# Reordered start of a fused image filter, transformer and attention kernel: loads, one tanh, and a step of VectorE's hand-written order

## The chip, the cores and the metric

The kernel runs on one core of a Trainium2 chip. A core has TensorE (PE in the profile, its weight loads PEld), VectorE (DVE), ScalarE (ACT), GpSimd (POOL) and SyncE (SP, which here only issues transfers). The metric is the time of one launch on the device in microseconds, the median of several runs.

## The reference, cut to what matters

Eight images of 256x256 go through ten iterations of a filter (`_L0_tok_ref`), eight token sequences of 128 go through a four-layer transformer (`_L0_txt_ref`), and the two results are joined and go through a windowed attention and a feed-forward block with spike counts. Only the first two concern the change. The filter, with `conv` meaning differences of neighbouring rows and columns:

```
u = sigmoid(o / EPS); q = 0
for _ in range(10):
    u_nabla = conv(u, nabla_w)
    q = maximum(q - TAU * (u_nabla[:, 0] * vf1 + u_nabla[:, 1] * vf0), 0)
    Tq = conv(stack([vf1 * q, vf0 * q]), div_w)
    u = sigmoid((o - Tq) / EPS)
return (o - Tq) / EPS
```

The transformer starts with `h = emb[x] + positional_encoding`. Each of its four blocks is softmax attention over 16 heads of width 16, a layer norm, a feed-forward part of width 1024 and a layer norm.

## The kernel before

Every engine has its own instruction list, written out by hand as a sequence of small named functions; semaphores tie the lists together. An engine works strictly in the order of its list, so a function whose inputs are late holds up all that stands behind it. That written order is what sets the order of the work everywhere in this case. There is no scheduler.

The images are handled in four pairs, two images at a time spread over 128 partitions with four rows each (`RPP`). One filter iteration `it` is this chain: ScalarE computes `u = tanh(...)` in `filter_out` (or `first_tanh` for the first iteration of a pair); VectorE takes column differences (`columns_apart`, L1715), weighs them with one component of the vector field (`columns_weighed`, L1721), takes row differences (`rows_apart`, L1726), advances q (`advance_columns`, L1739 in a pair's first iteration and L1743 later), weighs the rows (`rows_weighed`, L1732), and then does `advance_rows` (L1748), `flux_rows` (L1754), `flux_cols` (L1760), `divergence_columns` (L1765), `divergence_rows` (L1770), `divergence_both` (L1775) and `divergence_out` (L1779), which releases the next tanh. Rows that lie on another partition are fetched by small SBUF to SBUF copies on SP's queue: `rows_below` (L271) for u after each tanh, `rows_above` (L318) for the flux. `rows_apart` waits for the first, `divergence_rows` for the second.

The transformer runs 16 blocks, four layers by four pairs of sequences. Block k's attention (`a`) is interleaved with the feed-forward part of block k-1 (`f`) in `block_step`, and two filter iterations are woven into each block. The first block has no feed-forward part to go with and a list of its own, `first_step`, on each engine. In the attention, TensorE makes transposed h (`turn_attn`, L531), ScalarE copies it (`attn_in`, L1127), TensorE projects it (L546), ScalarE copies keys and queries (`keys_out`, `queries_out`, L1163), TensorE makes scores for two sets of 8 heads at a time (`scores`, L597), VectorE reduces each set to its maxima (`head_max(k, n)`, n = 0 to 3, L1784), ScalarE exponentiates (`exps(k, n, half)`, L1100), TensorE transposes the probabilities (`turn_probs`, L607) and multiplies by the values (`attend`, L619), VectorE takes `reciprocals` (L1788) of the sums, ScalarE spreads and copies them (`spread_rden`, `rden_out` L1121), VectorE multiplies (`normalise`, L1793), and TensorE projects the result out (`project_out`, L636). `scores(0, 1)` may start only when `exps(0, 1, 1)` is done. The next block begins with VectorE's `columns_apart`, `columns_weighed`, `moments_attn` (statistics of what `project_out` left) and `head_max(a, 0)`.

In the prologue SP loads tokens, the first images (`o_all`), and the vector field `vf` in two components: component 1, with which the columns are weighed (`l_vf`), and component 0, for the rows (`l_vf_rows`). ScalarE issues the loads of the filter taps and of the positional encoding `pe`. VectorE compares the taps with the expected ones and branches on the outcome. GpSimd gathers embedding rows into `h`: two gathers at once, then it waits for the projection weights `w_attn` (`l_qkv`) before the other six. When all gathers have landed (`g_emb`) SP issues the remaining weights of the first layer (`first_weights`, among them `w1` of 1 MB), and behind them in its list stands `rows_below(1)`.

At the end of a pair ScalarE writes the finished pair scaled by 0.5 to `f_out` (L1090), then computes the first tanh of the next pair from `o_all` (L1081).

## Time and profile before

| what | value |
|---|---|
| median of 3 runs | 996.21 us (996.08 to 999.59) |
| the profiled execution: its own time, its span | 997.71 us, 996.0 us |
| busy share of the span: PE, DVE, ACT, POOL | 92%, 84%, 70%, 12% |
| mean granted TensorE clock | 0.972 of full |
| chain that ended last, by engine | DVE 45%, PE 26%, ACT 17%, issue 8% |
| stretch of the first block (start to the third iteration's first difference) | 0 to 58.4 us |

The span runs from the first to the last instruction of the profiled execution; its own time is a little longer. A granted clock of 1 is 2.4 GHz, of 0.5 is 1.2 GHz. The busy share of PE is that of pipelined matmuls with modelled ends and does not mean that it runs at its peak. In rows of the timeline an end is start plus duration; two instructions of an engine can overlap by about 0.1 us, since the next starts while the last one's results drain.

### The profile page before, as it was taken

The page shows a single profiled execution, that of the slowest core. Times are in us where ns is not written, and L with a number is a line of the kernel's source. Part 1 is how long each engine was busy: PE and PEld are TensorE (multiplying, and loading weights), DVE is VectorE, ACT ScalarE, POOL GpSimd, SP SyncE. Part 2 cuts the span into 40 slices and gives each one's busy share as a digit, 9 for nine tenths or more (in the row PEclk, how much of TensorE's full clock was granted, in tenths as well). Part 3 has the DMA queues.
Part 4 walks back from the last instruction along what each step waited for, and adds up shares of the span by engine and source line. Part 5 has one row for each costly group of instructions (what it writes and reads, how often), then busy time and mean ns, then how long its engine had stood idle before and what let it go on. Part 6 is the DMA issues. An engine that isn't in the chain of part 4 may idle for free.

```text
span 996.0 us, 18934 instructions
## 1 busy us (share of the span) xinstructions
PE 912.3 (92%) x6988; PEld 708.9 (71%) x6988; DVE 833.2 (84%) x1160; ACT 699.2 (70%) x2252; POOL 119.2 (12%) x147
## 2 busy tenths in 40 slices
PE   6689999999999999989999999889998999999997
PEld 5467777777777777877777877767675766667675
DVE  4889999999999999999999998888799599452443
ACT  2766877876877877877876875757767686867842
POOL 4301011011011111101101111101011101000000
PEclk8699999999999999999999999799999999999999
DMA  5312030031010120010220010000001000100000
GB/s 141 91 72 61 32 112 17 27 117 48 17 43 17 45 81 35 17 47 13 70 80 11 17 38 11 12 11 23 27 17 35 20 23 11 49 27 2 17 1 32
DMA packets 24924, 39.00 MB, mean 39 GB/s; under 512 B 4000, under 2 KB 20608, under 8 KB 23552
## 3 DMA queue, kind: packets, MB, share of 16 engines
q1 hardware_dynamic: 24016, 36.59, 11.6%
q0 software_dynamic: 384, 1.05, 0.6%
q8 instruction: 56, 0.92, 0.4%
q14 instruction: 36, 0.29, 0.1%
q10 hardware_dynamic: 432, 0.15, 0.1%
HBM read 22.21 MB, written 5.24 MB: 28 GB/s over the span
## 4 chain that ended last, share of the span: by engine, by line
DVE 45%; PE 26%; ACT 17%; issue 8%; DMA 2%; POOL 1%; SPq 0%; DVEq 0%; POOLq 0%; ACTq 0%
ACT prob L1100 8%; PE ps_t L857 6%; PE ps_m L868 4%; DVE f L1775 4%; DVE f L1779 4%; DVE f L1748 4%; DVE f L1770 4%; DVE neg_max L1784 4%; DVE p L1760 4%; ACT u L1087 3%; DVE f L1765 3%; DVE f L1715 2%; DVE f L1732 2%; DVE f L1743 2%; DVE f L1721 2%
## 5 line engine op out<-in xcount | busy, mean ns | idle before, releaser
L1100 ACT ACTIVATE prob<-ps_s,neg_max 128x128 f32<-128x128 f32 x512 | 181.1, 406 | 3.3 <-DVE neg_max L1784 3.3
L1100 ACT ACTIVATION_READ_ACCUMULATOR prob<-ps_s,neg_max 128x1 f32 x512 | 126.1, 247 | 0.0
L661 PE MATMUL ps_t<-w,hidT 128*128 128x256 f32 x512 | 125.7, 383 | 0.0
L1108 ACT ACTIVATE probT<-ps_t 128x512 f32<-128x512 f32 x128 | 80.9, 632 | 47.5 <-PE ps_t L607 30.9
L661 PEld LDWEIGHTS ps_t<-w,hidT 128*128 128x128 f32 x512 | 91.0, 190 | 12.1 <-ACT hidT L1184 2.6
L857 PE MATMUL ps_t<-km,w_fc 128*128 128x384 f32 x256 | 91.6, 492 | 1.4 <-ACT km L1299 1.4
L607 PE MATMUL ps_t<-ident,prob 128*128 128x128 f32 x512 | 82.7, 286 | 8.9 <-ACT probT L1108 5.0
L607 PEld LDWEIGHTS ps_t<-ident,prob 128*128 128x128 f32 x512 | 61.5, 146 | 31.4 <-issue 13.0
L1784 DVE TENSOR_REDUCE neg_max<-ps_s 128x8 f32<-128x1024 f32 x64 | 77.5, 1212 | 3.8 <-PE ps_s L597 3.8
L1358 ACT ACTIVATE prob<-ps_s,neg_max 128x128 f32<-128x128 f32 x192 | 53.9, 376 | 26.2 <-DVE neg_max L1965 25.8
L650 PE MATMUL ps_t<-hT_f,w 128*128 128x256 f32 x256 | 65.7, 402 | 3.0 <-ACT hT_f L1112 3.0
L546 PE MATMUL ps_s<-hT_a,w_attn 128*128 128x256 f32 x256 | 66.8, 396 | 1.5 <-DMA w_attn<-in_w_attn 1.5
L857 PEld LDWEIGHTS ps_t<-km,w_fc 128*128 128x128 f32 x256 | 46.2, 190 | 26.1 <-ACT km L1299 1.9
L868 PE MATMUL ps_m<-w_pr,o_all 128*128 128x256 f32 x256 | 63.8, 385 | 0.0
L1715 DVE TENSOR_TENSOR f<-u 128x1024 f32<-128x1024 f32 x40 | 48.9, 1223 | 16.1 <-ACT u L1087 12.4
L1087 ACT ACTIVATE u<-f 128x1024 f32<-128x1024 f32 x36 | 38.1, 1057 | 34.2 <-DVE f L1779 34.1
L650 PE MATMUL ps_y<-hT_f,w 128*128 128x256 f32 x256 | 60.6, 379 | 0.0
L650 PEld LDWEIGHTS ps_t<-hT_f,w 128*128 128x128 f32 x256 | 50.1, 201 | 12.9 <-ACT hT_f L1112 6.1
L1142 ACT ACTIVATE h<-ps_y,shift_a,rstd_a 128x256 f32<-128x256 f32 x32 | 16.3, 562 | 55.4 <-DVE shift_a L1817 55.4
L546 PEld LDWEIGHTS ps_s<-hT_a,w_attn 128*128 128x128 f32 x256 | 46.6, 197 | 9.9 <-issue 3.2
L868 PEld LDWEIGHTS ps_m<-w_pr,o_all 128*128 128x128 f32 x256 | 46.1, 190 | 8.5 <-issue 1.0
L1726 DVE TENSOR_TENSOR f<-u 128x1024 f32<-128x1024 f32 x40 | 48.9, 1222 | 3.7 <-DMA u<-u 3.4
(179 smaller groups left out, 2046.1 us busy)
## 6 DMA issues: line engine op xcount, KB each, us to landing
w<-in_w SPq DMA_DIRECT2D x8, 1024.0 KB, 5.0
u<-u SPq DMA_DIRECT2D x80, 63.0 KB
p<-p SPq DMA_DIRECT2D x80, 63.0 KB
w_attn<-in_w_attn SPq DMA_DIRECT2D x4, 768.0 KB, 4.7
out<-w SPq DMA_DIRECT2D x7, 384.0 KB, 2.6
o_all<-in_o SPq DMA_DIRECT2D x4, 512.0 KB, 4.7
filtered<-f_out SPq DMA_DIRECT2D x4, 512.0 KB, 3.1
x<-filtered SPq DMA_DIRECT2D x8, 256.0 KB, 2.7
```

The lines of the kernel that those rows point to most:

```text
L546: last = mm(dst, w_attn[:, c, D * w + P * m:D * w + P * m + P], hT_a[:, k % 2, c], start=(c == 0), stop=(c == KC - 1))
L607: last = tr(ps_t[:, 1, P * hh:P * hh + P], prob[:, n % 2, 4 * half + hh], ident[:])
L650: last = mm(ff_banks[j % 2][:, D * (m % 2):D * (m % 2) + D], w1[:, c, P * m:P * m + P], hT_f[:, c], start=(c == 0), stop=(c == KC - 1))
L661: last = mm(ps_t[:, 0, D * t:D * t + D], hidT[:, m, P * t:P * t + P], w2[:, m], start=False, stop=(m == MC - 1), skip_group_check=True)
L857: last = mm(ps_t[:, m % 2, 0:TOK], w_fc[:, c, P * m:P * m + P], xn2T[:, c], start=(c == 0), stop=(c == KC - 1))
L868: last = mm(dst, hid_f[:, m, P * t:P * t + P], w_pr[:, m], start=(m == 0), stop=(m == MC - 1))
L1087: A(u[:, 0:RPP, 0:IMG], fa, ACT.Tanh, scale=0.25).then_inc(s["act_tanh"], 1)
L1100: last = A(prob[:, n % 2, hh], ps_s[n % 2][:, hh], ACT.Exp, scale=-1.0, bias=neg_max[:, n % 2, hh:hh + 1], accum_out=den)
L1108: A(probT[:, 4 * half:4 * half + 4].rearrange("p h k -> p (h k)"), ps_t[:, 1], ACT.Copy).then_inc(s["act_pT"], 1)
L1358: last = A(prob[:, t % 2, head], quad[hb][:, P * hh:P * hh + P], ACT.Exp, bias=neg_max[:, t, head:head + 1])
L1715: tt(fb, u[:, 0:RPP, 1:], u[:, 0:RPP, 0:IMG], ALU.subtract).then_inc(s["u_cols"], 1)
L1784: dve.tensor_reduce(neg_max[:, n % 2], ps_s[n % 2][:], AX.X, ALU.min).then_inc(s["dve_max"], 1)
```

## The change

Five edits, none of which changes what is computed or how many arithmetic instructions there are:

1. The two tap loads and the load of `pe` go from ScalarE's list to SP's: the taps stand ahead of the images, `pe` behind component 1 of the field.
2. The load of the projection weights `w_attn` stands ahead of component 0 of the field (the row field), no longer behind the first row copies.
3. ScalarE's explicit wait for GpSimd's constants ahead of the first tanh is gone.
4. In `first_step`, VectorE's `divergence_columns(0)` goes ahead of `head_max(0, 0)`; the first half of the second iteration (`columns_weighed(1)`, `rows_apart(1)`, `advance_columns(1)`) goes ahead of `head_max(0, 2)` and `head_max(0, 3)`; the two `normalise` go behind the whole divergence. ScalarE's `filter_out(0)` goes between the two halves of `exps(0, 1)`.
5. At the end of a pair the next pair's first tanh is computed before the copy to `f_out`. `rows_apart` of a pair's first iteration, which overwrites what the copy reads, gets a wait for the copy.

```diff
@@ -259,11 +259,20 @@
             sp.dma_start(tokens[:], d["tokens"]).then_inc(s["l_tok"], 16)
+            sp.dma_start(taps[:, 0:18], d["nabla_w"].partition_broadcast(P)).then_inc(s["l_taps"], 16)
+            sp.dma_start(taps[:, 18:36], d["div_w"].partition_broadcast(P)).then_inc(s["l_taps"], 16)
             load_images = lambda k: sp.dma_start(o_all[:, k], d["o"][2 * k:2 * k + 2].rearrange("b (p r) c -> (b p) r c", r=RPP))
             load_images(0).then_inc(s["l_img"], 16)
-            for comp, loaded in ((1, "l_vf"), (0, "l_vf_rows")):
+
+            def load_field(comp, loaded):
                 for img in range(2):
-                    sp.dma_start(vf[64 * img:64 * img + 64, comp], d["vf"][comp].rearrange("(p r) c -> p r c", r=RPP)).then_inc(s[loaded], 16)
+                    sp.dma_start(vf[64 * img:64 * img + 64, comp], d["vf"][comp].rearrange("(p r) c -> p r c", r=RPP)).then_inc(loaded, 16)
+
+            load_field(1, s["l_vf"])
+            sp.dma_start(pe[:], d["pe"]).then_inc(s["l_pe"], 16)
+            sp.dma_start(w_attn[:, :, 0:3 * D], d["w_attn"][0][:, :, 0:3 * D]).then_inc(s["l_qkv"], 16)
+            load_field(0, s["l_vf_rows"])
+
...
             sp.wait_ge(s["c_pool"], N_EARLY)
             rows_below(0)
-            sp.dma_start(w_attn[:, :, 0:3 * D], d["w_attn"][0][:, :, 0:3 * D]).then_inc(s["l_qkv"], 16)
...
-            act.dma_start(taps[:, 0:18], d["nabla_w"].partition_broadcast(P)).then_inc(s["l_taps"], 16)
-            act.dma_start(taps[:, 18:36], d["div_w"].partition_broadcast(P)).then_inc(s["l_taps"], 16)
-            act.dma_start(pe[:], d["pe"]).then_inc(s["l_pe"], 16)
...
                 else:
-                    act.wait_ge(s["st_img"], 16 * pair + 16)
-                    A(f_out[:], fa, ACT.Copy, scale=0.5).then_inc(s["act_img"], 1)
                     if pair + 1 < PAIRS:
                         act.wait_ge(s["l_img_rest"], 16 * (PAIRS - 1))
                         first_tanh(pair + 1)
+                    act.wait_ge(s["st_img"], 16 * pair + 16)
+                    A(f_out[:], fa, ACT.Copy, scale=0.5).then_inc(s["act_img"], 1)
...
                 exps(0, 1, 0)
+                filter_out(0)
                 exps(0, 1, 1)
                 probs_out(0, 1, 0)
-                filter_out(0)
                 probs_out(0, 1, 1)
...
-            act.wait_ge(s["c_pool"], N_EARLY)
             act.wait_ge(s["l_img"], 16)
             first_tanh(0)
...
             def rows_apart(it):
                 dve.wait_ge(s["act_tanh"], it + 1)
                 dve.wait_ge(s["halo_u"], 32 * it + 32)
+                if it and it % ITERS == 0:
+                    dve.wait_ge(s["act_img"], it // ITERS)
...
                 flux_cols(0)
+                divergence_columns(0)
                 head_max(0, 0)
-                divergence_columns(0)
                 head_max(0, 1)
...
                 columns_apart(1)
-                head_max(0, 2)
-                head_max(0, 3)
                 columns_weighed(1)
                 rows_apart(1)
                 advance_columns(1)
+                head_max(0, 2)
+                head_max(0, 3)
                 rows_weighed(1)
+                advance_rows(1)
                 reciprocals(0, 0)
-                advance_rows(1)
-                reciprocals(0, 1)
                 flux_rows(1)
                 flux_cols(1)
+                reciprocals(0, 1)
                 divergence_columns(1)
-                normalise(0, 0)
                 divergence_rows(1)
-                normalise(0, 1)
                 divergence_both(1)
                 divergence_out(1)
+                normalise(0, 0)
+                normalise(0, 1)
                 restart()
```

What the edits do to the compiled lists is shown at three places. First ScalarE's list from its start, before, with what each instruction waits for (`l_img` is the landing of the first images, `c_pool` GpSimd's constants):

```order
L1072 UNCONDITIONAL_BRANCH [waits barrier_Pool_Activation_PE_DVE_SP_release]
L1076 DMA taps<-in_nabla_w 128x18
L1077 DMA taps<-in_div_w 128x18
L1078 DMA pe<-in_pe 128x256
L1081 ACT_TABLE_LOAD [waits l_img]
L1081 ACTIVATE u<-o_all 128x4x256 [waits c_pool]
L1275 TENSOR_LOAD general [waits c_general]
```

And the same place in the changed kernel, where the first tanh is line 1085:

```order
L1080 UNCONDITIONAL_BRANCH [waits barrier_Pool_Activation_PE_DVE_SP_release]
L1085 ACT_TABLE_LOAD
L1085 ACTIVATE u<-o_all 128x4x256 [waits l_img]
L1278 TENSOR_LOAD general [waits c_general]
L1278 ISA x2
```

With two waits the compiler put that for the images on the table load and that for the constants on the tanh; with one wait it stands on the tanh, and the table load waits for nothing.

Second, SP's list from its start, before:

```order
L261 DMA tokens<-in_tokens 128x8
L262 DMA o_all<-in_o 128x1024
L266 DMA vf<-in_vf 64x1024 x4
L271 DMA u<-u 63x256 x2
L275 DMA w_attn<-in_w_attn 128x2x768
```

And in the changed kernel:

```order
L261 DMA tokens<-in_tokens 128x8
L262 DMA taps<-in_nabla_w 128x18
L263 DMA taps<-in_div_w 128x18
L264 DMA o_all<-in_o 128x1024
L269 DMA vf<-in_vf 64x1024 x2
L272 DMA pe<-in_pe 128x256
L273 DMA w_attn<-in_w_attn 128x2x768
L269 DMA vf<-in_vf 64x1024 x2
L280 DMA u<-u 63x256 x2
```

Two small loads now stand ahead of the images, and the projection weights stand ahead of two of the four field loads and of the row copies.

Third, VectorE's list in the first step, from the second iteration's column differences on, before (`f` is any of the filter's work tiles):

```order
L1715 TENSOR_TENSOR f<-u 128x1024
L1784 TENSOR_REDUCE neg_max<-ps_s 128x8 x2
L1721 TENSOR_TENSOR f<-f,vf 128x1024
L1726 TENSOR_TENSOR f<-u 128x1024
L1743 SCALAR_TENSOR_TENSOR f<-f 128x1024
L1732 TENSOR_TENSOR f<-f,vf 128x1024
```

And in the changed kernel, where these lines are 3 to 5 higher:

```order
L1718 TENSOR_TENSOR f<-u 128x1024
L1724 TENSOR_TENSOR f<-f,vf 128x1024
L1731 TENSOR_TENSOR f<-u 128x1024
L1748 SCALAR_TENSOR_TENSOR f<-f 128x1024
L1789 TENSOR_REDUCE neg_max<-ps_s 128x8 x2
L1737 TENSOR_TENSOR f<-f,vf 128x1024
```

The two maxima of the third and fourth head sets moved behind the row differences and the advance of the columns.

## Rows read from the trace of the kernel before

**Rows 1.** The page: shares by engine of the chain that ended last.
```profile
DVE 45%; PE 26%; ACT 17%; issue 8%; DMA 2%; POOL 1%; SPq 0%; DVEq 0%; POOLq 0%; ACTq 0%
```

**Rows 2.** That chain, 0 to 130 us: start us, us, what.
```profile
12.39 4.63 DMA w_attn<-in_w_attn
...
17.15 5.99 PE ps_s L546 x16
...
31.08 1.40 ACT prob L1100 x8
...
57.33 1.06 ACT u L1087
```

**Rows 3.** Timeline, 0 to 17 us: start us, us, engine line operation, idle before.
```profile
8.21 1.28 ACT L1081 ACT_TABLE_LOAD   x1 [8.21 <-DMA o_all<-in_o]
...
15.72 0.60 ACT L1127 ACTIVATE hT_a<-ps_s 128x512 f32<-128x512 f32 x1 [5.16 <-PE ps_s L531]
...
11.93 1.23 DVE L1721 TENSOR_TENSOR f<-f,vf 128x1024 f32<-128x1024 f32 x1
...
13.96 0.69 DVE L1704 TENSOR_TENSOR h<-h,pe 128x512 f32<-128x512 f32 x1
...
14.71 0.92 PE L531 MATMUL ps_s<-ident,h 128*128 128x128 f32 x4 [4.57 <-DVE h L1704]
```

**Rows 4.** Transfers issued at 2.3 (last of two), 7.1 and 30.9 us: last number us to landing.
```profile
vf<-in_vf SPq DMA_DIRECT2D x2, 256.0 KB, 7.7
...
h<-in_emb,tok_idx POOLq DMA_INDIRECT x1, 6.1
...
w<-in_w SPq DMA_DIRECT2D x1, 1024.0 KB, 6.1
```

**Rows 5.** Timeline, 25 to 39 us, SP, ACT and DVE.
```profile
28.73 0.61 SPq L344 DMA_DIRECT2D w_attn<-in_w_attn  x1
...
38.82 0.37 ACT L1100 ACTIVATE prob<-ps_s,neg_max 128x128 f32<-128x128 f32 x1 [0.47 <-DVE neg_max L1784]
...
25.03 1.23 DVE L1784 TENSOR_REDUCE neg_max<-ps_s 128x8 f32<-128x1024 f32 x1 [3.85 <-PE ps_s L597]
...
36.42 1.23 DVE L1715 TENSOR_TENSOR f<-u 128x1024 f32<-128x1024 f32 x1 [2.42 <-ACT u L1087]
37.57 2.35 DVE L1784 TENSOR_REDUCE neg_max<-ps_s 128x8 f32<-128x1024 f32 x2
```

**Rows 6.** Timeline, 49 to 62 us, ACT, DVE and PE.
```profile
52.83 0.42 ACT L1121 ACTIVATE rden<-ps_s 128x256 f32<-128x256 f32 x1
...
61.77 1.19 DVE L1784 TENSOR_REDUCE neg_max<-ps_s 128x8 f32<-128x1024 f32 x1
...
55.10 1.89 PE L636 MATMUL ps_y<-w_attn,attnT 128*128 128x256 f32 x8
58.92 1.74 PE L597 MATMUL ps_s<-km,qT 32*128 32x256 f32 x16 [1.93 <-ACT qT L1163]
```

**Rows 7.** The chain again, at a row copy that ended a wait.
```profile
613.76 1.06 ACT u L1087
...
615.58 2.19 DMA u<-u
```

**Rows 8.** Timeline, 198 to 216 us, at the end of the first pair.
```profile
203.63 1.06 ACT L1090 ACTIVATE f_out<-f 128x1024 f32<-128x1024 f32 x1 [0.93 <-DVE f L1779]
...
204.60 1.04 ACT L1081 ACTIVATE u<-o_all 128x1024 f32<-128x1024 f32 x1
...
205.74 1.23 DVE L1715 TENSOR_TENSOR f<-u 128x1024 f32<-128x1024 f32 x1 [1.41 <-ACT u L1081]
```

**Rows 9.** Waits of DVE, 57 to 560 us: us in total, times, longest.
```profile
DVE f L1715 <- ACT u L1081: 2.7, 2, 1.4
```

**Rows 10.** Sums over stretches: us, PE busy (instructions), granted clock, DMA share, GB/s.
```profile
15.00:21.80 6.80, 5.28 (x15) 0.50 0.31 100
...
618.00:640.00 22.00, 17.98 (x156) 0.77 0.02 7
```

## The prediction

> **What bounds the kernel now.** I read the page first, for the engines' shares of the chain that ended last: VectorE has 45% of it and TensorE 26% [rows 1], so neither alone is the limit, and a reordering counts only where the chain runs through what it moves. I then followed the chain in order of time. In the prologue it goes through transfers: the first images, the tanh, the projection weights (landed at 12.39 + 4.63 = 17.02), the projections at 17.15 [rows 2]. In the first block it goes to the third head set's maxima and the exponentials behind them, then through ScalarE and TensorE, and at 57.33 to the tanh of the second iteration [rows 2], 4 us later than ScalarE could have computed it, since its copy of the sums was done at 52.83 + 0.42 = 53.25 [rows 6]. From there on, through the text blocks, it is mostly VectorE's own list with a tanh between iterations. So a lead that all three engines have at the start of block 1 is carried to the end, and a lead of VectorE alone is not. That is what I work out: at what time the three can start block 1.
>
> **The prologue.** ScalarE's table load waits for the images and takes 1.28 us (8.21 to 9.49) ahead of the tanh [rows 3]; in the changed list it waits for nothing and is over long before. The images are issued two tap loads later, some 0.9 us (I estimate this from SP's 0.4 to 0.6 us for an issue, such as the 0.61 of [rows 5]), but no longer share the engines with the taps and `pe`; I take 8.6 instead of 8.2 for their landing (bounds 8.2 and 9.1), so the tanh ends at 9.7 and the column differences start at 9.75. Weighing them needs component 1 of the field. Its two parts landed on average 7.7 us after issues up to 2.3 [rows 4], the later one thus at 10.0 or after; it too is issued 0.9 later, so I take 11.3 (bounds 10.0 and 12.2). From the start of that weighing to `positions_first` is 13.96 - 11.93 = 2.03 us of VectorE's work [rows 3]: 11.3 + 0.05 + 2.03 = 13.4. The second gather landed at 7.15 + 6.1 = 13.25 [rows 4] and nothing of it is moved, which gives the same 13.4. So `positions_first` gains about 0.55 us, not the 1.3 of the table load.
>
> From `positions_first` to the projections are 0.75 us to the transposes, 1.01 to the copy, 0.60 for it and 0.05: 15.72 + 0.60 + 0.05 - 13.96 = 2.41 [rows 3], that is 15.8, if the weights are there. Before they were issued at 12.39; now at about 5, behind 1 MB of images and field and `pe`. Alone they took 4.6 us [rows 2]. I estimate 14.0: before, the same queue had finished images and both components by about 12.6, and the weights put 0.25 MB more in the place of the row component and start 0.9 later (bounds 13.0 and 15.5, both before 15.8). So the projections start at 15.8 and not at 17.15: 1.35 us gained. The row component now lands behind the weights, near 16; `rows_weighed(0)` stands 2.3 us behind `positions_first`, at 15.8, and VectorE had 3.85 us of idle time ahead of the first maxima [rows 5] that hide a delay of it, less the 1.2 that `divergence_columns(0)` now takes of them and the 0.8 by which TensorE gained more than VectorE. Cover left is 1.8 us.
>
> **The first step's list.** The first maxima start at 25.03 - 1.35 = 23.7 [rows 5]. `divergence_columns(0)` lies in idle time ahead of them, so the divergence is complete at 23.7 + 2 x 1.15 + 3 x 1.25 = 29.75. ScalarE's first half of `exps(0, 1)` ended at 31.08 + 1.40 = 32.48 [rows 2], now at 31.1, and the tanh follows at once and ends at 32.1, where before it let VectorE start only at 36.42 [rows 5]. The price is a tanh (1.05) ahead of the other half of these exponentials; TensorE's `scores(0, 1)` wait for them, but end near 35.5, and their maxima are not asked for before 37.4.
>
> What asks for them late is the new order on VectorE. `rows_apart(1)` needs the row copies. Where such a copy ended a wait, it landed at 615.58 + 2.19 = 617.77, 2.95 us after its tanh ended at 614.82 [rows 7]. So VectorE works 2.5 us on the columns, idles 0.45, starts the row differences at 32.1 + 2.95 = 35.05, and after two operations of 1.2 the third set's maximum at 37.4 (before 37.57 [rows 5]). The exponentials behind it start at 38.65 instead of 38.82. Of the 1.35 us of lead 0.2 is left here: the new order spends the rest.
>
> It comes back at the end of the step. The exponentials keep ScalarE and TensorE in turn until the second copy of the sums at 53.25 - 0.2 = 53.05 [rows 6]. VectorE meanwhile ends the maxima at 39.7 and does the eight remaining operations of the iteration and the two reciprocals, waiting once for exponentials and once for the flux's row copies, by about 50.2, all in time in which it waited before. So the tanh runs from 52.95 to 54.0 instead of ending at 58.39 [rows 2], and the column differences start at 54.05 (before 58.42): 4.4 us for VectorE. The `normalise` pair, put behind the divergence, finds VectorE idle and waits only for ScalarE's copies, as before. TensorE's `project_out` starts at 54.9 (before 55.10), held by the work ahead of it; the scores can follow after 1.82 at 56.7, since the queries are copied by 54.6; before, they waited for that copy until 58.92 [rows 6]. They take 1.15 us at full clock, as at other block starts, or 1.74 as here [rows 6], and end at 57.9 or 58.4. VectorE is through column weights and statistics at 57.8. So block 1's first maxima start at 57.9 and not at 61.77 [rows 6]: 3.9 us gained, 3.4 with the slower scores. I take 3.9, as TensorE no longer idles ahead of them. The next wait there, ScalarE's for the layer norm's shift, depends on VectorE and moves with it, and so does TensorE behind that: all three have the lead.
>
> **The pair ends.** Copy and tanh ran from 203.63 to 205.64, and VectorE, idle for 1.41 us, started at 205.74 [rows 8]. It was free at 204.33; a tanh that starts at 203.63 and takes 1.04 lets it start at 204.74: 1.0 gained. The copy's end stays at 205.7, and `rows_apart`, which now waits for it, stands at 209 or later, so that wait costs nothing; if it had to follow the tanh at once it would cost 1.0. The queries' copy on ScalarE keeps its place behind both. VectorE waited so at two pair ends, 2.7 us in all [rows 9]; at the third the list of waits has no such entry, and I count nothing. That is 2.0 us.
>
> **The sum.** 3.9 + 2.0 = 5.9 us. Against the profiled execution (997.71 with a span of 996.0) that is 991.8; that execution lies 1.5 above the median, so for the median 996.21 - 5.9 = 990.3.
>
> **A rule that speaks against the change.** The row copies of the second iteration are now asked for at 32.1, not at 36.3, and `first_weights` puts `w1` on the same queue ahead of them. Before, these loads started at 28.73 [rows 5], 11.7 us after the projection weights had landed, and `w1` landed at 30.9 + 6.1 = 37.0 [rows 4], 20.0 us after them. With 14.0 for the weights that gives 25.7 and 34.0, a us before the row copies land in my sum. So I charge nothing; each us that the weights land after 15 costs one. The Trainium skill, DMA: Bandwidth & Descriptors, section Queues, rings and completion order, says that on each DMA engine descriptors are consumed in ring order. By that rule nothing overtakes `w1`, and the rival below is as dear as I price it; were the copies free to overtake, it would cost nothing.
>
> **Rivals.** (a) The forecast, chance 0.50: 990.3, own range 988.8 to 992.0. (b) The prologue gives nothing, because field, gather or weights land late, 0.15: the exponentials then start 1.15 later than before, the block start gains 3.9 - 1.35 = 2.55, and with 2.0 the time is 991.7. For it: only 0.55 us of the table load's 1.28 passes my own estimates of landings. Against it: the weights waited at 17.02 for nothing but their late issue. (c) The lead at block 1 is lost again, because TensorE has its own full list there, 0.10: only the pair ends count, 994.2. Against it: the chain before goes through VectorE there. (d) The row copies stand behind `w1`, 0.07: if it lands at 37.0 as before, they land some 3.3 late, and 993.6 is left. (e) The same mechanism makes the kernel slower, 0.05: from a landing of the copies at 41 on (35.05 + 5.9) the maxima behind them eat the whole gain, at 42 the time is 997.2; the weights would have to land later than they did before. (f) More is gained, 0.13: the granted clock was 0.50 from 15 to 21.8 [rows 10], and the 16 projections took 5.99 us [rows 2]; at full clock 8 of the same kind take 1.89 [rows 6], so 16 about 3.8. With TensorE less idle ahead of them 2.2 more may come: 988.1. The same clock works the other way too: from 618 to 640 it was 0.77 [rows 10] where TensorE bounds, and a few us at half clock more or fewer there move the time by 1 to 2 us; this is in the ranges.
>
> **How the numbers follow.** About 0.5% (5 us) is what a measurement of this kernel can tell from no change; the bound is 991.2. Of (a) three quarters lie under it, all of (f) and a third of (b): 0.375 + 0.13 + 0.05 = 0.555 for faster, rounded to 0.56. Only a part of (e) is over 1001: 0.02. The rest, 0.42, is within. The range from 987.2 to 994.6 holds (a) to (c) but for tails, most of (d) and of (f), and leaves out (e).
>
> **What would show it.** In the changed profile: the table load in the first 3 us; the projections at 15.8; the first tanh of block 0's filter ending at 32 with a VectorE wait for a row copy behind it; the third set's maximum near 37.4; the second tanh ending at 54.0; the maxima of block 1 at 57.9; no wait of VectorE for ScalarE of over 1.2 us at the pair ends. I would be wrong if the row copies landed later than 35.5, if the weights landed after 15.8, or if the difference at 58 us were not found again at 560.

## The result and the profile after

| | median | executions |
|---|---|---|
| changed kernel | 993.77 us | 12 |
| kernel before, on the same chip | 996.62 us | 12 |
| ratio | 0.9953, 95% interval 0.9935 to 0.9970 | |

By the ratio the change saves 4.7 us of 996.6 (3.0 to 6.5): by the bound of 0.5% it lies just inside "no change", and the interval shows that there is one. The two medians lie only 2.9 us apart, a little outside that interval; here and in the runs below the ratio, which has the interval, gives 0.5 to 2.2 us more than the difference of the medians. The forecast was 5.9 us. The profiled execution of the changed kernel took 995.07 us with a span of 993.3, that of before 997.71 with 996.0.

The page's shares of the chain that ended last have hardly moved from [rows 1]:

```profile
DVE 46%; PE 25%; ACT 16%; issue 9%; DMA 2%; POOL 1%; SPq 0%; DVEq 0%; POOLq 0%; ACTq 0%
```

What the change does shows in the timeline of its prologue (start us, us, engine line operation, idle before), beside [rows 3]:

```profile
0.80 1.28 ACT L1085 ACT_TABLE_LOAD   x1 [0.80 <-PEq L2245]
...
4.56 0.60 SPq L273 DMA_DIRECT2D w_attn<-in_w_attn  x1
...
7.21 1.06 ACT L1085 ACTIVATE u<-o_all 128x1024 f32<-128x1024 f32 x1 [5.13 <-DMA o_all<-in_o]
...
9.68 1.23 DVE L1724 TENSOR_TENSOR f<-f,vf 128x1024 f32<-128x1024 f32 x1 [0.16 <-DMA vf<-in_vf]
...
14.30 0.69 DVE L1707 TENSOR_TENSOR h<-h,pe 128x512 f32<-128x512 f32 x1 [2.62 <-DMA h<-in_emb,tok_idx]
...
16.39 1.22 DVE L1731 TENSOR_TENSOR f<-u 128x1024 f32<-128x1024 f32 x1 [1.39 <-DMA u<-u]
```

The table load is over at 2.08, the tanh starts at 7.21 (before 9.51), the column field is there at 9.7 and not at the expected 11.3. All of this lead is then spent in one wait: `positions_first` (L1707) waits 2.62 us for a gather and starts at 14.30, later than the 13.96 of before. The chain that ended last goes through that gather now, and not through the weights as in [rows 2] (start us, us, what):

```profile
5.95 8.28 DMA h<-in_emb,tok_idx
...
16.46 6.72 PE ps_s L554 x16
...
33.94 0.77 SPq L280
...
34.75 2.18 DMA u<-u
```

The gather was issued 1.2 us earlier than before and took 8.28 us where [rows 4] have 6.1. The projections start at 16.46 (before 17.15) and take 6.7 us, 0.7 longer than before; by the granted clock, TensorE is at half clock for 6.8 us there in both traces, before from 15.0 to 21.8 and now from 15.7 to 22.5, so that only the last 0.7 us of the projections (before 1.3) ran at full clock. The first step in the timeline, beside [rows 5] and [rows 6]:

```profile
25.07 2.35 DVE L1789 TENSOR_REDUCE neg_max<-ps_s 128x8 f32<-128x1024 f32 x2 [0.81 <-PE ps_s L605]
...
32.84 1.08 ACT L1091 ACTIVATE u<-f 128x1024 f32<-128x1024 f32 x1
...
37.02 1.22 DVE L1731 TENSOR_TENSOR f<-u 128x1024 f32<-128x1024 f32 x1 [0.53 <-DMA u<-u]
...
39.30 2.35 DVE L1789 TENSOR_REDUCE neg_max<-ps_s 128x8 f32<-128x1024 f32 x2
40.55 0.37 ACT L1104 ACTIVATE prob<-ps_s,neg_max 128x128 f32<-128x128 f32 x1 [1.42 <-DVE neg_max L1789]
...
54.13 0.42 ACT L1125 ACTIVATE rden<-ps_s 128x256 f32<-128x256 f32 x1
...
54.40 1.10 ACT L1091 ACTIVATE u<-f 128x1024 f32<-128x1024 f32 x1
...
59.44 1.23 DVE L1789 TENSOR_REDUCE neg_max<-ps_s 128x8 f32<-128x1024 f32 x1
```

The first maxima start where they did before (25.07 against 25.03), the third set's 1.7 us later than before, and block 1's 2.3 us earlier. The end of the first pair, beside [rows 8]:

```profile
201.12 1.06 ACT L1085 ACTIVATE u<-o_all 128x1024 f32<-128x1024 f32 x1 [0.93 <-DVE f L1784]
202.09 1.04 ACT L1097 ACTIVATE f_out<-f 128x1024 f32<-128x1024 f32 x1
202.28 1.23 DVE L1718 TENSOR_TENSOR f<-u 128x1024 f32<-128x1024 f32 x1 [0.46 <-ACT u L1085]
```

VectorE's idle time there fell from 1.41 to 0.46. The list of its waits from 57 to 560 us has 0.9 us in the place of the 2.7 of [rows 9] (us in total, times, longest):

```profile
DVE f L1718 <- ACT u L1085: 0.9, 2, 0.5
```

A good way to see where a lead is won and lost is to subtract the start of the same instruction in two traces. I took VectorE's maxima in the text blocks and, from 658 us on, one addition in each window of the later part. Lead over before in us, at before's time; the last column is the difference of the spans:

```
                      25    38    62   209   393   430   597   658   880   end
changed              0.0  -1.7   2.3   3.5   5.0   4.5   4.5   6.9   4.4   2.7
e1_prologue          1.2   1.2   1.4   1.4   1.7   1.8   1.9   1.8   1.8   1.8
e2_first_step       -0.6  -3.4  -0.4  -0.2   0.7   0.9   0.9   1.5  -1.2  -1.2
e3_pair_ends         0.3   0.3   0.3   1.3   2.7   2.9   2.9   5.0   0.7   0.7
e4_again             1.0  -0.3   2.6   3.7   5.6   5.8   5.8   7.1   4.9   5.0
e5_weights_behind   -0.7  -2.4   0.1   1.2   2.9   3.1   3.1   4.3   2.2   2.2
e6_weights_wait     -0.8  -2.5   1.3   2.4   2.6   2.8   2.8   5.3   5.1   5.1
e7_maxima_early      1.0   1.6   5.0   6.1   6.2   6.4   6.3   8.9   8.7   8.7
e8_both              0.2   0.7   4.1   5.2   6.5   5.8   5.8   8.2   5.7   4.0
e9_early_again       1.2   1.8   5.3   6.3   8.2   7.7   7.7   8.2   5.4   5.4
e10_early_wait_field 0.5   0.5   4.1   5.2   6.8   7.3   7.2   7.4   4.5   4.5
```

Behind 600 us no edit has changed anything, yet the leads move by up to 4.3 us between two columns, and by up to 2.7 from 597 us to the end. TensorE's clock goes with it: from 600 to 640 us the granted clock was 0.87 before and 0.91 in the changed kernel, whose lead grows by 2.4 us until 658; that the one makes the other is not shown. The changed kernel's lead falls from 6.6 us at 835 to 4.4 at 880, where its clock was below full and before's was not. Sums over 836 to 848 us (PE, weight loads, VectorE, ScalarE and GpSimd busy, granted clock, DMA share, GB/s), first the changed kernel:

```profile
836.00:848.00 12.00, 9.88 (x57) 6.03 (x58) 9.45 (x18) 8.43 (x22) 0.39 (x2) 0.72 0.27 98
```

and the same stretch of the kernel before:

```profile
836.00:848.00 12.00, 9.33 (x71) 6.14 (x69) 11.02 (x17) 9.31 (x18) 2.79 (x2) 1.00 0.03 13
```

So one profile against another can't size an edit of 1 us from the end of the program. I read leads at 62, 209, 393 and 597 us, and total times from ratios. Even there the table has noise: from 209 to 386 us, where no edit differs, the leads moved by -0.9 (e6, e7) to +0.9 us (e2, e4).

### The profile page after: what moved, and what is told of

Read it like the earlier page. It is cut to its first block, busy times and chain, and to the rows that moved or that the text cites. A ratio compares the mean times of both kernels' runs of the same rounds, so it can differ in the third digit from the quotient of the medians.

```text
span 993.3 us, 18933 instructions
## 1 busy us (share of the span) xinstructions
PE 911.6 (92%) x6988; PEld 705.3 (71%) x6988; DVE 833.9 (84%) x1160; ACT 699.0 (70%) x2252; POOL 122.2 (12%) x147
## 4 chain that ended last, share of the span: by engine, by line
DVE 46%; PE 25%; ACT 16%; issue 9%; DMA 2%; POOL 1%; SPq 0%; DVEq 0%; POOLq 0%; ACTq 0%
ACT prob L1104 8%; PE ps_t L865 6%; DVE f L1753 4%; DVE neg_max L1789 4%; PE ps_m L876 4%; DVE f L1780 4%; DVE f L1784 4%; DVE f L1775 4%; DVE p L1765 4%; ACT u L1091 3%; DVE f L1770 3%; DVE f L1748 2%; DVE f L1718 2%; DVE f L1737 2%; DVE f L1724 2%
## 5 line engine op out<-in xcount | busy, mean ns | idle before, releaser
L865 PE MATMUL ps_t<-km,w_fc 128*128 128x384 f32 x256 | 95.1, 508 | 1.0 <-ACT km L1302 1.0
L615 PE MATMUL ps_t<-ident,prob 128*128 128x128 f32 x512 | 82.0, 284 | 10.1 <-ACT probT L1112 5.1
L554 PE MATMUL ps_s<-hT_a,w_attn 128*128 128x256 f32 x256 | 67.5, 400 | 0.8 <-ACT hT_a L1131 0.8
L658 PE MATMUL ps_t<-hT_f,w 128*128 128x256 f32 x256 | 62.1, 386 | 3.8 <-ACT hT_f L1116 3.8
L1091 ACT ACTIVATE u<-f 128x1024 f32<-128x1024 f32 x36 | 38.1, 1059 | 32.8 <-DVE f L1784 32.4
L658 PEld LDWEIGHTS ps_t<-hT_f,w 128*128 128x128 f32 x256 | 47.3, 190 | 13.2 <-ACT hT_f L1116 7.4
L554 PEld LDWEIGHTS ps_s<-hT_a,w_attn 128*128 128x128 f32 x256 | 47.1, 199 | 9.0 <-issue 3.0
L1780 DVE TENSOR_TENSOR f<-f 128x1024 f32<-128x1024 f32 x40 | 48.9, 1222 | 3.7 <-issue 0.3
```

Source lines behind the costliest of these rows:

```text
L554: last = mm(dst, w_attn[:, c, D * w + P * m:D * w + P * m + P], hT_a[:, k % 2, c], start=(c == 0), stop=(c == KC - 1))
L615: last = tr(ps_t[:, 1, P * hh:P * hh + P], prob[:, n % 2, 4 * half + hh], ident[:])
L658: last = mm(ff_banks[j % 2][:, D * (m % 2):D * (m % 2) + D], w1[:, c, P * m:P * m + P], hT_f[:, c], start=(c == 0), stop=(c == KC - 1))
L865: last = mm(ps_t[:, m % 2, 0:TOK], w_fc[:, c, P * m:P * m + P], xn2T[:, c], start=(c == 0), stop=(c == KC - 1))
L1091: A(u[:, 0:RPP, 0:IMG], fa, ACT.Tanh, scale=0.25).then_inc(s["act_tanh"], 1)
L1780: tt(fa, fa, fb, ALU.add).then_inc(s["div_rc"], 1)
```

## The experiments

### The change in three parts

**e1_prologue** has edits 1 to 3 (loads, table load) in the kernel before, and nothing else.

```diff
+            sp.dma_start(taps[:, 0:18], d["nabla_w"].partition_broadcast(P)).then_inc(s["l_taps"], 16)
...
+            load_field(1, s["l_vf"])
+            sp.dma_start(pe[:], d["pe"]).then_inc(s["l_pe"], 16)
+            sp.dma_start(w_attn[:, :, 0:3 * D], d["w_attn"][0][:, :, 0:3 * D]).then_inc(s["l_qkv"], 16)
+            load_field(0, s["l_vf_rows"])
...
-            act.wait_ge(s["c_pool"], N_EARLY)
```

> Only edits 1 to 3 (loads and the wait ahead of the first tanh), the order of the first step and of the pair ends as before. Theory (after the result): the second gather gates positions_first near 14.3 and the projections run at half clock, so the first maxima start at 25.0 +- 0.7, block 1's first maxima at 61.8 +- 0.7 (before 61.77) and the time does not move by over 1 us on that account. Rival: the prologue carries a good part of the gain and the first step only passes it on; then block 1's first maxima start 1.3 us or more earlier.

Measured: 996.70 beside 997.79 us, ratio 0.9982 (0.9968 to 0.9996): 1.8 us. VectorE's rows of its timeline show the same late gather:

```profile
13.94 0.69 DVE L1707 TENSOR_TENSOR h<-h,pe 128x512 f32<-128x512 f32 x1 [2.22 <-DMA h<-in_emb,tok_idx]
...
23.84 1.22 DVE L1787 TENSOR_REDUCE neg_max<-ps_s 128x8 f32<-128x1024 f32 x1 [1.20 <-PE ps_s L605]
```

TensorE's rows show a quicker set of projections:

```profile
16.56 5.38 PE L554 MATMUL ps_s<-hT_a,w_attn 128*128 128x256 f32 x16 [0.75 <-ACT hT_a L1131]
```

The projections start 0.6 us earlier than before, not 1.35. That the maxima gain 1.2 is due to 5.38 us of projections in place of 5.99. Block 1's maxima start at 60.34, 1.4 us earlier than before: my expectation of 61.8 +- 0.7 missed, and the rival's 1.3 us is there, 0.6 of it from the quicker projections.

**e2_first_step** has edit 4 alone, in the kernel before.

```diff
                 exps(0, 1, 0)
+                filter_out(0)
                 exps(0, 1, 1)
...
-                head_max(0, 2)
-                head_max(0, 3)
                 columns_weighed(1)
                 rows_apart(1)
                 advance_columns(1)
+                head_max(0, 2)
+                head_max(0, 3)
```

> Only edit 4 (VectorE's order and the tanh amid the exponentials in the first step). The weights are then issued at 28.7 as before and w1 lands at 37.0, while the row copies of the second iteration are asked for near 33.5. Theory (ring order): the copies stand behind w1 and land at 37.7 to 38.5 instead of 36.4, so that the third set's maximum starts near 40.5 and block 1's first maxima at 60.5 to 61.0, a lead of only about 1 us where the whole change has 2.3. Rival: the copies overtake w1, land 3.0 us after the tanh near 36.4, and the lead is 2.5 to 3 us.

Measured: 997.57 us, ratio 0.9990 (0.9971 to 1.0008): nothing that can be told from noise. The new order has no lead at block 1 without the early weights (-0.4 us, expected about 1), and the trace says why. Its chain, at the row copies of the second iteration:

```profile
33.06 0.96 ACT u L1087
...
34.84 3.71 DMA u<-u
```

and its timeline on SP and VectorE:

```profile
30.96 0.43 SPq L348 DMA_DIRECT2D w<-in_w  x1
...
38.65 1.22 DVE L1726 TENSOR_TENSOR f<-u 128x1024 f32<-128x1024 f32 x1 [2.06 <-DMA u<-u]
```

The last of the row copies took 3.71 us from its issue, and landed 4.5 us after the tanh's end (34.02), where the changed kernel has 2.18 and 3.0. `w1` was issued at 30.96 and took 7.2 us, until 38.1; the copies, issued at 34.04, landed just behind it. That is rival (d), in the kernel where it applies. VectorE waits 2.06 us, the maxima behind the copies start at 40.93, 3.4 us later than before, and block 1 has no lead left. The Trainium skill (DMA: Bandwidth & Descriptors, section Queues, rings and completion order) says that each DMA engine consumes a queue's descriptors in ring order, though a later one may finish its write before an earlier one; this trace agrees with the order, 38.1 for `w1` and 38.6 for the copies behind it.

**e3_pair_ends** has edit 5 alone.

```diff
-                    act.wait_ge(s["st_img"], 16 * pair + 16)
-                    A(f_out[:], fa, ACT.Copy, scale=0.5).then_inc(s["act_img"], 1)
                     if pair + 1 < PAIRS:
                         act.wait_ge(s["l_img_rest"], 16 * (PAIRS - 1))
                         first_tanh(pair + 1)
+                    act.wait_ge(s["st_img"], 16 * pair + 16)
+                    A(f_out[:], fa, ACT.Copy, scale=0.5).then_inc(s["act_img"], 1)
...
+                if it and it % ITERS == 0:
+                    dve.wait_ge(s["act_img"], it // ITERS)
```

> Only edit 5 (the next pair's tanh ahead of the copy, a wait of rows_apart for the copy). Theory: nothing differs until 203 us; from there the lead is 1.0 us, from the second pair end on 2.0, at the third nothing is added. VectorE's wait for ScalarE at these two ends falls from 1.4 to 0.4 us. Rival: the wait for the copy holds up rows_apart, and the lead at 400 us is under 1 us.

Measured: 995.68 us, ratio 0.9974 (0.9957 to 0.9990): 2.6 us. Its lead grows by 1.0 at 206 us (0.3 to 1.3) and by 1.0 at 390 (1.7 to 2.7), and by nothing at the third pair end at 575 (2.9 before it and behind it). This term stood in the forecast at 2.0.

**e4_again** is the changed kernel once more, in the same series.

> The changed kernel itself once more, for a second trace. Theory: up to 620 us the starts agree with the first trace within 0.7 us, block 1's first maxima at 59.4; what differs behind that comes with stretches of half clock of TensorE in the fusion part, and moves the end by up to 3 us either way. Rival: the lead of 4.5 us at 600 us is itself luck of the first trace; then the two traces differ by over 1.5 us at 600 us already.

Measured: 992.79 us, ratio 0.9938 (0.9915 to 0.9961): 6.2 us, where the first measurement had 4.7. The three parts alone make 1.8 + 1.0 + 2.6 = 5.4 us. At block 1, where only the first two and their meeting count, they have 1.4 - 0.4 = 1.0 and the whole has 2.3 and 2.6: the two need each other. The clock in the projections differs between these traces, so count from the first maxima: block 1's follow 36.7 us later before, 36.5 in e1 and in e2, and 34.4 and 35.1 in the two traces of the changed kernel. The trace of this execution has the first maxima at 24.04 and the third set's at 37.84, near my 23.7 and 37.4, and still block 1 starts at 59.18. TensorE's clock takes the difference. Its timeline here:

```profile
47.28 1.09 PE L615 MATMUL ps_t<-ident,prob 128*128 128x128 f32 x4
48.30 1.08 PE L627 MATMUL ps_s<-probT,v 128*32 128x128 f32 x16
49.31 1.91 PE L554 MATMUL ps_s<-hT_a,w_attn 128*128 128x256 f32 x4
```

and in the first profile of the changed kernel:

```profile
48.73 1.09 PE L615 MATMUL ps_t<-ident,prob 128*128 128x128 f32 x4
49.75 0.67 PE L627 MATMUL ps_s<-probT,v 128*32 128x128 f32 x16
50.34 1.13 PE L554 MATMUL ps_s<-hT_a,w_attn 128*128 128x256 f32 x4
```

The same 20 matmuls end at 51.2 and 51.5, though one started 1.45 us before the other. The windows around them show the granted clock (columns as above), in the second measurement:

```profile
48.00:50.00 2.00, 2.00 (x20) 1.20 (x19) 1.86 (x3) 0.72 (x2) 0.00 (x0) 0.50 0.99 416
50.00:52.00 2.00, 2.00 (x11) 1.69 (x10) 0.70 (x1) 0.42 (x2) 0.00 (x0) 0.77 0.43 174
```

and in the first:

```profile
50.00:52.00 2.00, 2.00 (x26) 1.54 (x19) 1.97 (x2) 0.64 (x2) 0.00 (x0) 1.00 0.97 401
```

From 50 us on the first ran at full clock and the second, for a while yet, at half.

### Why the second gather is late

**e5_weights_behind** puts the weights behind component 0 of the field. I had blamed the weights for the late gather.

```diff
             sp.dma_start(pe[:], d["pe"]).then_inc(s["l_pe"], 16)
+            load_field(0, s["l_vf_rows"])
             sp.dma_start(w_attn[:, :, 0:3 * D], d["w_attn"][0][:, :, 0:3 * D]).then_inc(s["l_qkv"], 16)
-            load_field(0, s["l_vf_rows"])
```

> The changed kernel with the projection weights issued behind the row component of the field (still ahead of the row copies). Theory: in the changed kernel the weights share the DMA engines with the second gather, which landed at 14.2 us although it was issued 1.2 us earlier than before; with the field there instead it lands at 12 to 13.3, the weights at 14.5 to 15.5, the projections start at 15.0 to 15.7 (changed kernel 16.5 to 16.7), and block 1's first maxima come 0.8 to 1.3 us earlier. Rival: what delays the gather is the load on the DMA engines whatever is loaded (2.4 MB in the first 15 us in either order); then the second gather lands near 14 again and the projections start at 16.3 to 16.7.

Measured: 995.51 beside 997.59 us, ratio 0.9966 (0.9942 to 0.9991); one of its ten executions took 2278.68 us, which the ratio leaves out and for which I have no cause. The gather did not come earlier, but later:

```profile
14.69 0.69 DVE L1707 TENSOR_TENSOR h<-h,pe 128x512 f32<-128x512 f32 x1 [2.98 <-DMA h<-in_emb,tok_idx]
```

So my theory in that form is wrong: it is not the weights as such. The same bytes are on the DMA engines in another order, and the gather waits as long. The projections start at 17.30, later even than the rival had it.

**e6_weights_wait** lets SP wait for both gathers before it issues the weights and component 0; all else is the changed kernel.

```diff
             sp.dma_start(pe[:], d["pe"]).then_inc(s["l_pe"], 16)
+            sp.wait_ge(s["g_emb_first"], 32)
             sp.dma_start(w_attn[:, :, 0:3 * D], d["w_attn"][0][:, :, 0:3 * D]).then_inc(s["l_qkv"], 16)
```

> The changed kernel in which SP waits for the first two gathers before it issues the projection weights and then the row component. Theory: with nothing but the column component beside them the gathers land at 10.5 to 12, positions_first starts with them, and the weights, issued then, land about 4 us later at 15 to 16: the projections start near 15.5. Rival: the gathers take their 7 to 8 us from issue to landing for another reason than the traffic, and land at 13.5 to 14 again.

Measured: 992.65 us in one execution, span 990.9. Its timeline:

```profile
5.94 0.95 POOL L434 DMA_INDIRECT h<-in_emb,tok_idx  x1 [0.30 <-issue]
...
10.10 0.60 SPq L274 DMA_DIRECT2D w_attn<-in_w_attn  x1
...
15.52 6.09 PE L555 MATMUL ps_s<-hT_a,w_attn 128*128 128x256 f32 x16 [2.63 <-DMA w_attn<-in_w_attn]
...
18.08 1.22 DVE L1732 TENSOR_TENSOR f<-u 128x1024 f32<-128x1024 f32 x1 [5.91 <-DMA u<-u]
...
25.87 2.35 DVE L1790 TENSOR_REDUCE neg_max<-ps_s 128x8 f32<-128x1024 f32 x2
```

The gather issued at 5.94 had landed when SP went on, at 10.1: some 4.1 us, where it took 8.28 with 1.25 MB issued about it (the weights at 4.56, the row field from 5.21). The issues of both gathers (KB, median us to landing), first in this run and then in the changed kernel:

```profile
h<-in_emb,tok_idx POOLq DMA_INDIRECT x2, 4.6
```

```profile
h<-in_emb,tok_idx POOLq DMA_INDIRECT x2, 8.1
```

With e5 this settles what delayed them: load from another queue, whatever it carries. The Trainium skill (the same page and section) says that a DMA engine takes turns between the queues that have work for it, a packet at a time; a transfer that was issued first is by that rule not served alone. The first gather of the changed kernel agrees with it: issued at 4.43, just ahead of the weights, it took 7.9 us, and 5.1 in e6. The projections start 0.9 us earlier than in the changed kernel, though they now wait 2.63 us for the weights. But the row copies, last in SP's queue, end a wait at 18.08 (in the changed kernel at 16.39), and VectorE needs 7.8 us from there to the first maxima: they start 0.8 us later than before. VectorE's rows are late next.

### What the late maxima cost

**e7_maxima_early** keeps the changed kernel but for the third and fourth head sets' maxima, which go ahead of the row differences.

```diff
                 columns_weighed(1)
+                head_max(0, 2)
+                head_max(0, 3)
                 rows_apart(1)
                 advance_columns(1)
-                head_max(0, 2)
-                head_max(0, 3)
```

> The changed kernel with head_max(0, 2) and head_max(0, 3) ahead of rows_apart(1) and advance_columns(1) (behind columns_weighed(1)). Theory: in the changed kernel the third set's maximum waits behind the row copies and costs 1.8 us of ScalarE's idle time; here it starts right behind scores(0, 1), 1.5 to 1.9 us earlier relative to the first maxima, and block 1's first maxima come as much earlier, since VectorE still ends the iteration before ScalarE is free. Rival: the exponentials then run before VectorE has the divergence, the tanh waits for it, and the gain at block 1 is under 0.7 us.

Measured: 991.57 beside 997.59 us, ratio 0.9930 (0.9903 to 0.9957). Block 1's maxima start at 56.76, 2.4 us earlier than in the second trace of the changed kernel, whose first maxima start at nearly the same time (24.04, here 24.00). Part of these 2.4 us are the matmuls at half clock shown above for e4: counted from the first maxima, block 1 follows after 32.8 us here and after 34.4 in the first trace of the changed kernel, so the order is worth 1.6 to 2.4 us. The four matmuls of L554 behind the exponentials take 1.13 us in all four traces with early maxima and in the first of the changed kernel, but 1.91 in e4 and 2.08 in e5; whether the late maxima have a part in that half clock was not tried. The maxima wait for their scores now and for nothing else:

```profile
35.99 2.36 DVE L1789 TENSOR_REDUCE neg_max<-ps_s 128x8 f32<-128x1024 f32 x2 [1.01 <-PE ps_s L605]
```

**e8_both** joins this with the load order of e5.

> Both: weights behind the row component and the maxima ahead of the rows. Theory: the two gains add, 2.5 to 3 us at block 1's first maxima against the changed kernel, and the time is 0.7 to 0.8% under the kernel before. Rival: one limit takes the place of the other (row copies behind w1, since the weights and so the other gathers and w1 come later while the tanh comes earlier), and block 1 gains under 2 us.

Measured: 992.80 us, ratio 0.9930 (0.9904 to 0.9956). The lead at block 1 is 4.1, 0.9 less than that of e7. The expectation of two gains had fallen with e5: its load order is a loss here too. The projections start at 17.30, 0.7 us later than in e7, as they did in e5 (0.6 to 0.8 later than in the changed kernel); that e5 alone lost more by block 1, 2.2 to 2.5 us, goes with longer half clock: four matmuls of L554 took 2.08 us in it at 51 us, and 1.13 here.

**e9_early_again** is e7 once more.

> The version with the late maxima ahead of the row differences once more, to see whether its ratio of 0.993 to before stands. My theory (the maxima of the third and fourth head sets wait in the changed kernel for row copies that they do not need, which costs 2.4 us): a ratio of 0.992 to 0.9935, 990 us beside a before of 997.5, the block-1 maxima again near 56.8 and a lead of 6 us at 600 us. Rival: the gain seen was the TensorE clock's doing in that execution; the ratio is then that of the changed kernel, 0.9945, and the lead at 600 us under 5.

Measured: 989.59 beside 998.94 us, ratio 0.9889 (0.9863 to 0.9914). Lead 5.3 at block 1 and 7.7 at 597. It has the lowest ratio of all, though e10's is not told from it: it is better than before in both series, by 7.0 and by 11.1 us of their ratios. Those differ by more than my expectation for it allowed, and its interval does not reach the 0.9930 of e7, though the two intervals meet (0.9903 to 0.9914); the table shows the late part of the program move by as much from one profile to the next, but that this makes the difference of the two ratios is not shown.

**e10_early_wait_field** adds to it a wait of SP for component 1 of the field ahead of the weights, on the same chip as e9.

```diff
             sp.dma_start(pe[:], d["pe"]).then_inc(s["l_pe"], 16)
+            sp.wait_ge(s["l_vf"], 32)
             sp.dma_start(w_attn[:, :, 0:3 * D], d["w_attn"][0][:, :, 0:3 * D]).then_inc(s["l_qkv"], 16)
```

> As the run beside it, and SP waits for component 1 of the field before it issues the projection weights and component 0. Theory (what is issued behind a gather before it lands makes it late): the gathers land by 12 instead of 14, transposed h is ready by 13.5, the weights are issued at about 9.4 and land at 14.6, so the projections start at about 14.7 instead of 16.6. But the row copies stand behind both and land at about 17.3, a us later than in the changed kernel, and VectorE needs 7.8 us from them to the first maxima, which start at 25.1: VectorE is late next, nothing is gained over the run beside it, and up to 1.1 us is lost. Rival: the first maxima hang on TensorE alone; they then start at 22.5 and the time is 1.5 us under the run beside it.

Measured: 990.70 us, ratio 0.9906 (0.9880 to 0.9931). The timeline:

```profile
11.09 0.69 DVE L1708 TENSOR_TENSOR h<-h,pe 128x512 f32<-128x512 f32 x1
...
14.61 5.15 PE L555 MATMUL ps_s<-hT_a,w_attn 128*128 128x256 f32 x16 [2.12 <-DMA w_attn<-in_w_attn]
...
16.78 1.23 DVE L1732 TENSOR_TENSOR f<-u 128x1024 f32<-128x1024 f32 x1 [5.00 <-DMA u<-u]
...
20.44 1.15 PE L606 MATMUL ps_s<-km,qT 32*128 32x256 f32 x16 [0.69 <-ACT qT L1168]
...
24.57 2.35 DVE L1790 TENSOR_REDUCE neg_max<-ps_s 128x8 f32<-128x1024 f32 x2
```

`h` is there at 11.09 without a wait, the projections start 1.9 us earlier than in e9, and the scores are done at 21.6. Nothing comes of it (its ratio and that of e9 can't be told apart): VectorE is busy with the first iteration, which started with the row copies at 16.78, until 24.57. In e9 the maxima started at 23.79. The prologue has two chains of nearly one length, and this wait shortens one at the price of the other, as expected.

## Why the prediction was right and wrong

**The whole.** 993.77 lies in the range from 987.2 to 994.6, 3.5 us above the forecast; the direction was right. Of the 5.9 us, 4.7 (3.0 to 6.5) and 6.2 (3.9 to 8.5) were measured, intervals that hold 5.9, so the total alone would not have shown the error. The traces do: the forecast had 3.9 us at the block's start and 2.0 at the pair ends, and they show 2.3 to 2.6 and 2.0. That the total comes so near is in part luck: in the second trace 0.9 us of the lead at 597 us came between 209 and 386, where no edit is, and by the medians the two measurements have 2.9 and 5.0 us.

**The pair ends, 2.0 us: right.** 0.9 to 1.0 at two of them, nothing at the third, in every trace of a kernel with edit 5.

**The step that failed: "The second gather landed at 7.15 + 6.1 = 13.25 [...] and nothing of it is moved".** The gather itself was moved, since tokens, and so indices, were there earlier and it was issued at 5.95; and the load around it was moved, since the weights and the row field now stand on the DMA engines while it runs. It landed at 14.2. I had counted 0.55 us gained at `positions_first`; it lost 0.34. That I had the images (8.6, landed 7.2) and the column field (11.3, landed 9.7) too late did not matter, since the gather hid both. With the gather at 14.2, much of rival (b) came true, which gave 2.55 us for the block's start and 991.7 for the whole. The start of the projections: 0.7 us gained of 1.35, and in the seven traces of kernels that load as the changed one or as e5, between -0.15 and 0.7. The weights, landed at 4.56 + 10.0 = 14.6 (expected 14.0), were not the bound.

**A second bound that the prediction left out** is the first row copies. In the new order they stand behind the weights and the row field in SP's queue, and end a wait of VectorE at 16.39; before, it had them without a wait:

```profile
14.57 1.22 DVE L1726 TENSOR_TENSOR f<-u 128x1024 f32<-128x1024 f32 x1
```

I had counted a cover of 1.8 us ahead of the first maxima and only the row field against it. VectorE's idle time there was 0.81 us, so it was free at 25.07 - 0.81 = 24.26 (in the second trace at 24.04 - 0.73 = 23.31). By the first trace the maxima would have started later than my 23.7 even with the gather in time; by the second they could just have kept to it. In e6 and e10, which start the projections at 15.5 and 14.6, it is this bound that holds the first maxima.

**The clock in the projections: a size I held fixed.** I let them take the 5.99 us of before. They took 6.71 in the first trace of the changed kernel and 5.43 in the second. So the first maxima came 1.37 and 0.34 us after my 23.7. Start (0.66) and duration (0.72) make up the 1.37 of the first.

**From there the chain kept its lengths, but for matmuls at half clock.** The maxima at 37.4 became 39.30: 1.37 from the first maxima, 0.45 from ScalarE, which waited for transposes at half clock ahead of the tanh. Row copies 2.95 us after a tanh became 3.0. They landed at 36.9, later than the 35.5 that I had named as a sign of being wrong; the tanh ahead of them ended 1.8 us late, and the mechanism was as said. From the exponentials to the second copy of the sums I had 38.65 to 52.63, 14.0 us; measured were 13.6 and, with the slow matmuls shown above, 14.8. From that copy's start to block 1's maxima I had 5.3; measured were 5.3 and 5.3. So 59.44 in place of 57.9 is 1.9 us of late start, less 0.4.

**"The new order spends the rest": right, and dearer than it needed to be.** I had seen that the row copies hold up the third set's maxima and did not ask what it costs: e7 shows 1.6 to 2.4 us. Where my own text kept 0.2 us of lead it stood beside a gain as large as that of the two pair ends.

**The rule that spoke against it: right about the rule, right that it costs nothing here.** e2 has the mechanism at full size: the copies 4.5 us after the tanh, the block start gone. With the weights early, `w1` is issued 2 us earlier (28.91) and is done at 35.9, a us ahead of the copies. So edits 1 to 3 and edit 4 are worth 1.0 us at block 1 apart and 2.3 to 2.6 together.

**Rival (f)** foresaw that TensorE with less idle time might get a better clock. In the first trace it did not: the granted clock from 25 to 58 us was 0.69 (before 0.74), and half clock lasted 6.8 us in the projections as before. Behind 600 us the leads change by up to 2.7 us either way until the end; at 838 us the clock goes with it. What decides when a stretch of half clock begins stays open.

## What to carry to other kernels

Moving a load forward moves every other transfer that is in flight then, those of other queues too: list them with their landings before you call one "not moved", and look for the one whose consumer is waiting. When a reordering puts an instruction behind one that waits for a transfer, price what its own consumer loses, even if the sum stays positive; the cheaper order was two instructions away. And where a kernel's end moves by microseconds between executions, subtract starts of the same instruction at a place behind the edit but ahead of that noise, and count from one place of the chain to the next.

## What was unexpected in the hardware

A gather of 128 rows issued at 5.95 took 8.3 us with 1.25 MB issued on another queue about it, and 4.1 us (e6) when nothing more was issued there until it had landed. With the taps and `pe` no longer issued by ScalarE, the 4 KB of tokens issued at 0.80 landed after 1.61 us, and the gather that needs them was issued 1.2 us earlier than before (5.95 against 7.15); which of the moved loads had held the tokens up was not tried. The same instructions of the same kernel ran at half clock in stretches that differ from execution to execution by 6.8 us and more (the changed kernel has one at 838 us in one trace and none in the other), with a lead 2.2 us smaller behind it.
